# First recurrent part: inverse rows on GpSimd, unscaled keys, plain value transposes, centred outputs, a split last inverse level, new orders

## The reference

```python
q, k, v = silu(conv4(xn @ W))            # causal depthwise convolution of 4 taps, each
k = k * 128 ** -0.5
alpha, beta = sigmoid(xn @ Wa + ba), sigmoid(xn @ Wb + bb)
def step(S, t):                          # S: batch x head x 128 x 128
    err = S k_t - v_t
    S = alpha_t * S - beta_t * err k_t^T
    return S, S q_t
o = (o - mean(o)) * rsqrt(var(o) + 1e-5) * ln_w + ln_b     # over the 128 values of a head
out = (o * sigmoid(xn @ Wg)) @ Wo
```

## Time and profile before

| | |
|---|---|
| median of 3 runs | 3200.43 us |
| profiled execution | 3194.02 us, span 3192.2 us |
| granted clock, mean | 0.995 |
| busy over the span | TensorE 97%, VectorE 69%, ScalarE 50%, GpSimd 30% |
| chain that ended last | TensorE 81%, VectorE 9%, GpSimd 4%, without a seen wait 3%, ScalarE 2% |
| recurrence of layer 0 | about 400 to 1875 us |

### The profile page before, as it was taken

The page is one execution under the profiler, slowest core; times in us unless marked ns, Lnnn a source line. Parts: engine busy times, 40 slices in busy tenths (PEclk is TensorE's granted clock), DMA queues, the critical chain, the costliest instruction groups (busy, mean ns, idle before and its releaser), DMA issues.

```text
span 3192.2 us, 61403 instructions
## 1 busy us (share of the span) xinstructions
PE 3112.1 (97%) x24240; PEld 2595.8 (81%) x24240; DVE 2204.3 (69%) x4430; ACT 1583.7 (50%) x3464; POOL 949.7 (30%) x1359
## 2 busy tenths in 40 slices
PE   8999989999999999999999989999999999999999
PEld 6888878888888888888888878778888888888887
DVE  6112288888888888888888843665666676666666
ACT  4221356766676667766766653344343333222222
POOL 2322313323332333233323234422323332222212
PEclk9999999999999999999999999999999999999999
DMA  2100211112111111111111145411010111000004
GB/s 91 30 20 27 68 54 48 41 48 54 45 41 53 52 48 42 48 54 45 41 54 51 30 157 158 140 43 30 27 30 27 30 43 30 27 20 27 24 17 158
DMA packets 130241, 165.69 MB, mean 52 GB/s; under 512 B 9937, under 2 KB 72145, under 8 KB 129921
## 3 DMA queue, kind: packets, MB, share of 16 engines
q1 hardware_dynamic: 120592, 144.49, 15.1%
q10 hardware_dynamic: 9296, 17.04, 1.5%
q0 software_dynamic: 64, 0.23, 0.0%
HBM read 127.91 MB, written 33.82 MB: 51 GB/s over the span
## 4 chain that ended last, share of the span: by engine, by line
PE 81%; DVE 9%; POOL 4%; issue 3%; ACT 2%; DMA 1%; DVEq 0%; ACTq 0%; SPq 0%; POOLq 0%
PE bank L71 21%; PE bank L73 21%; PE bank L72 21%; PE bank L932 3%; DVE b_zt L1430 3%; PE bank L1045 2%; PE bank L1071 2%; PE bank L1055 2%; PE bank L944 2%; PE bank L1070 1%; PE bank L1030 1%; PE bank L1020 1%; PE bank L1081 1%; DVE b_MN L1500 1%; POOL b_ss L1708 1%
## 5 line engine op out<-in xcount | busy, mean ns | idle before, releaser
L1430 DVE SCALAR_TENSOR_TENSOR b_zt<-b_rx,b_cw,b_zt 128x512 f32<-128x512 f32 x576 | 483.7, 840 | 29.7 <-ACT b_zt L1193 9.7
L71 PE MATMUL bank<-b_XH,b_wh 128*128 128x512 f32 x1024 | 465.4, 455 | 0.0
L72 PE MATMUL bank<-b_XL,b_wh 128*128 128x512 f32 x1024 | 404.0, 395 | 0.0
L73 PE MATMUL bank<-b_XH,b_wl 128*128 128x512 f32 x1024 | 403.4, 394 | 0.0
L71 PE MATMUL bank<-b_XH,b_qh 128*128 128x512 f32 x1024 | 399.3, 390 | 1.4 <-DVE b_g L2540 1.4
L72 PE MATMUL bank<-b_XL,b_qh 128*128 128x512 f32 x1024 | 398.7, 389 | 0.0
L73 PE MATMUL bank<-b_XH,b_ql 128*128 128x512 f32 x1024 | 398.6, 389 | 0.0
L2639 POOL TENSOR_TENSOR b_QHL<-b_qhd,b_QHH 128x512 fp32r<-128x512 f32 x128 | 181.8, 1424 | 476.6 <-ACT b_QHH L2418 474.2
L2418 ACT CAST b_QHH<-b_qhd 128x512 fp32r<-128x512 f32 x128 | 79.5, 623 | 308.0 <-PE bank L73 186.4
L73 PEld LDWEIGHTS bank<-b_XH,b_wl 128*128 128x128 f32 x1024 | 192.6, 188 | 43.6
L71 PEld LDWEIGHTS bank<-b_XH,b_qh 128*128 128x128 f32 x1024 | 192.5, 188 | 41.6 <-DVE b_g L2540 1.9
(11 more groups left out here) (248 smaller groups left out, 7596.7 us busy)
## 6 DMA issues: line engine op xcount, KB each, us to landing
b_abc<-tmp_a SPq DMA_DIRECT2D x64, 256.0 KB, 4.0
b_gbc<-tmp_g SPq DMA_DIRECT2D x64, 256.0 KB, 3.7
tmp_og<-b_gg SPq DMA_DIRECT2D x64, 256.0 KB, 2.3
b_mo<-tmp_og SPq DMA_DIRECT2D x64, 256.0 KB, 3.2
b_wr<-in_Wk SPq DMA_DIRECT2D x16, 256.0 KB, 4.3
b_wr<-in_Wq SPq DMA_DIRECT2D x16, 256.0 KB, 3.0
b_wr<-in_Wv SPq DMA_DIRECT2D x16, 256.0 KB, 2.9
b_wr<-in_Wg SPq DMA_DIRECT2D x16, 256.0 KB, 3.0
```

Source lines behind the costliest of these rows:

```text
L71: e.do.matmul(out, wh, xh, start=first and k == 0, stop=False)
L72: e.do.matmul(out, wh, xl, start=False, stop=False)
L73: m = e.do.matmul(out, wl, xh, start=False, stop=last and k == n - 1)
L1430: e.do.scalar_tensor_tensor(out=z[:, :], in0=rx[:, j:j + 512], scalar=cw[:, u // 2, KIND[name[0]], j:j + 1], in1=z[:, :], op0=ALU.mult, op ...
```

## The change

- rows moves from VectorE to GpSimd, unchanged.
- Keys are left without the factor 128 ** -0.5: finish writes them straight to KQA, scaled_k goes, and the step sizes are scaled by 1/128 in the stage ahead instead.
- The values are transposed only; the mean is taken from the outputs: ScalarE's copy of the outputs is two activations with a sum each, sums squares the centred values through scale and bias, mean (GpSimd) divides the sums, and scaled subtracts and multiplies, in four operations a batch instead of one.
- inverse7 and inverse8 are done in three calls: 7 for chunks 0 to 3; 8 for 0 to 3 and 7 for 4 to 7 in turn; 8 for 4 to 7. out7 is in two halves.
- The orders of all five engines in a round, the banks and the lags are new. g1 is projected a round later; the decay of queries and off_diagonal a round (by its index) sooner.

```diff
-PROJECTIONS = (("v1", 1), ("g0", 2), ("k0", 0), ("v0", 0), ("g1", 2), ("q0", 0), ("k1", 0), ("q1", 0))
+PROJECTIONS = (("g1", 3), ("q0", 1), ("k1", 1), ("q1", 1), ("v1", 1), ("g0", 2), ("k0", 0), ("v0", 0))
 
 TURNS = (
-    ("sc0", 1, 0), ("s6", 2, 3), ("s7", 2, 3), ("sc1", 1, 1), ("turn0", 3, 0), ("sc2", 1, 3),
-    ("s8", 2, 2), ("sc3", 1, 1), ("turn1", 3, 2), ("kv3", 2, 1), ("kv0", 1, 0), ("kv1", 1, 0),
-    ("kv2", 1, 3), ("s3", 1, 0), ("s4", 1, 0), ("s5", 1, 1),
+    ("kv0", 2, 2), ("kv1", 2, 1), ("kv2", 2, 0), ("s3", 2, 1), ("s4", 2, 1), ("s5", 2, 0),
+    ("s6", 2, 2), ("sc0", 1, 3), ("s7a", 2, 0), ("s78", 2, 2), ("sc1", 1, 1), ("sc2", 1, 3),
+    ("turn0", 3, 0), ("kv3", 2, 1), ("sc3", 1, 2), ("turn1", 3, 0),
...
-            m = e.do.matmul(kb[:, x * 256 + 128:x * 256 + 256], t[f"vt{b}"][:, (c0 + x) * 128:(c0 + x + 1) * 128], cmat,
-                            start=True, stop=True)
+            m = e.do.transpose(kb[:, x * 256 + 128:x * 256 + 256], t[f"vt{b}"][:, (c0 + x) * 128:(c0 + x + 1) * 128], ident)
...
+    def inverse7(u, m):
+
+        return e.do.matmul(bank[BANK["s7a"]][64:128, m * 64:m * 64 + 64], X[0:64, m, 64:128], NF[0:64, m, :], start=True, stop=True)
+
+    def inverse8(u, m):
+        return e.do.matmul(bank[BANK["s78"]][0:64, m * 64:m * 64 + 64], Z2[64:128, m, :], t[f"MF{u % 2}"][64:128, m, 64:128],
+                           start=True, stop=True)
+
+    def inverse7_first(u):
+        if not live(u):
+            return
+        bank_free(e, "s7a", u)
         e.wait_ge("mfc", 6 * u + 2)
         e.wait_ge("mfd", 3 * u + 3)
-        for m in range(8):
-            r = e.do.matmul(bank[BANK["s7"]][64:128, m * 64:m * 64 + 64], X[0:64, m, 64:128], NF[0:64, m, :], start=True, stop=True)
+        for m in range(4):
+            r = inverse7(u, m)
         r.then_inc(S["s7"], 1)
 
-    def inverse8(u):
-        if not live(u):
-            return
-        bank_free(e, "s8", u)
-        e.wait_ge("z2", u + 1)
+    def inverse78(u):
+
+        if not live(u):
+            return
+        bank_free(e, "s78", u)
+        e.wait_ge("z2", 2 * u + 1)
         e.wait_ge("mfc", 6 * u + 6)
-        e.wait_ge("mfd", 3 * u + 3)
-        for m in range(8):
-            r = e.do.matmul(bank[BANK["s8"]][0:64, m * 64:m * 64 + 64], Z2[64:128, m, :], t[f"MF{u % 2}"][64:128, m, 64:128],
-                            start=True, stop=True)
+        for m in range(4):
+            inverse8(u, m)
+            r = inverse7(u, m + 4)
+        r.then_inc(S["s7"], 1)
+
+    def inverse8_second(u):
+        if not live(u):
+            return
+        e.wait_ge("z2", 2 * u + 2)
+        for m in range(4, 8):
...
-            e.do.activation(z[:, :], z[:, :], ACT.Silu, bias=bias).then_inc(S["ksil"], 1)
+            e.wait_ge("p1", chain_step(u - 2, 3)[1])
+            e.do.activation(KQA[:, u % 2, b, :, :], z[:, :].rearrange("p (c t) -> p c t", c=4), ACT.Silu, bias=bias).then_inc(S["kq"], 1)
...
-        e.do.copy(t["OS"][:, :, ch, :], bank[7][:, 0:256].rearrange("p (b t) -> p b t", b=2)).then_inc(S["oc"], 1)
+        for b in range(2):
+            i = 4 * b + ch
+            e.do.activation(t["OS"][:, b, ch, :], bank[7][:, b * 128:b * 128 + 128], ACT.Copy,
+                            accum_out=t["ss"][:, 3, i:i + 1]).then_inc(S["oc"], 1)
...
-            e.do.activation(t["sq"][:, :], t["OS"][:, b, ch, :], ACT.Square,
-                            accum_out=t["ss"][:, 0, i:i + 1]).then_inc(S["sqs"], 1)
+            e.do.activation(t["sq"][:, :], t["OS"][:, b, ch, :], ACT.Square, scale=-128.0,
+                            bias=t["ss"][:, 3, i:i + 1], accum_out=t["ss"][:, 0, i:i + 1]).then_inc(S["sqs"], 1)
...
-    def scaled_k(u, b):
-        if not live(u):
-            return
-        e.wait_ge("ksil", 2 * u + b + 1)
-        e.wait_ge("p1", chain_step(u - 2, 3)[1])
-        e.do.tensor_scalar(KQA[:, u % 2, b, :, :], t[f"zt{(6 * u + 3 * b) % 2}"][:, :].rearrange("p (c t) -> p c t", c=4),
-                           KS, None, ALU.mult).then_inc(S["kq"], 1)
...
-        e.do.tensor_tensor(t["OS"][:, b, :, :], t["OS"][:, b, :, :], ss[:, 2, b * 4:b * 4 + 4].unsqueeze(2).to_broadcast([128, 4, 128]),
-                           ALU.mult).then_inc(S["osc"], 1)
+        e.wait_ge("mu", u + 1)
+        for ch in range(4):
+            i = 4 * b + ch
+            r = e.do.tensor_scalar(t["OS"][:, b, ch, :], t["OS"][:, b, ch, :], ss[:, 4, i:i + 1], ss[:, 2, i:i + 1], ALU.subtract, ALU.mult)
+        r.then_inc(S["osc"], 1)
...
+        e.do.tensor_scalar(ss[:, 4, :], ss[:, 3, :], 1.0 / 128, None, ALU.mult).then_inc(S["mu"], 1)
...
```

More of the change, by code:

```diff
@@ new lines, in attn0_pe @@
+        project(i - 1, "k1", 0, 1)
+        project(i - 1, "q0", 1, 2)
+        chain1(i - 3, 3)
+        ahead(i - 3, 2)
+        project(i - 1, "q0", 2, 3)
+        project(i - 1, "k1", 1, 2)
+        project(i - 1, "q0", 3, 4)
+        chain2(i - 3, 3)
+        ahead(i - 3, 3)
+        project(i - 1, "k1", 2, 3)
+        turn_kv(i - 2, 2)
+        project(i - 1, "k1", 3, 4)
+        chain4(i - 3, 3)
+        project(i - 1, "q1", 0, 1)
+        chain3(i - 3, 3)
+        ahead(i - 3, 4)
+        inverse3(i - 2)
```

353 lines of the change are left out of this document (173 added, 180 removed), and 6 rows, old and new, of tables (EMPTIED, SEMAPHORES).

## The result

The changed kernel takes 3222.39 us (median; 3220.09 to 3225.61) against 3200.2 us: a ratio of 1.0059 with a 95% interval of 1.004 to 1.0079. It is slower, by about 22 us, or 0.6%, where 46 us less had been forecast. The profiled execution took 3221.71 us with a span of 3219.9.

What follows compares the result with a forecast made beforehand. TensorE (98% busy) was taken as the bound. New work 42.25 us plus 1.8 of stall gives a period of 44.05 against 45.48, -46 us over 32 rounds: 3149 us, with 8 in 10 from 3095 to 3230.

Steps and rivals of the forecast that it cites:

- TensorE's saved work: Value transposes 0.9 us less a round, inverse7 and inverse8 interleaved 0.25 less: 1.15 x 32 = 37 us.
- Its whole work: TensorE's instructions in one round summed to 43.4 us before the change and 42.25 after it.
- The rows on GpSimd: The 30 row operations on GpSimd take 15.0 us a round, plus 0.8 for halo and tail copies.
- 1.4 us of new stall a round before inverse3: On TensorE: rows and copies want 15.8 us where 14.4 are left, so inverse3 waits.
- Rival B: GpSimd becomes the bound, rows at 25 us delay spread, blocks and inverse3: 3344 us; chance 0.17.
- about 2.1 us of each round is TensorE waiting: Kernel before: round of 45.48 us less 43.4 of work, mostly waits before the outputs' turn and third scores.
- the old stall: TensorE's wait before scores 2 for masked, behind scaled and the root: 0.4 us a round stays.
- I take nothing: VectorE's scaled as eight operations for two: bounds -0.7 to +0.9 us a round, priced at no change.
- Filling and draining: Start and end of the kernel: 35 rounds in both, the round starts elsewhere; plus or minus 8 us.
- C: Rival: cuts eaten by waits at ScalarE or slow rows, 3178 to 3207 us; chance 0.13 together with D.
- D: Rival: interleaved batch doesn't overlap, value transposes no cheaper, 3194 us; chance 0.13 together with C.
- A: Rival: rows at 11.4 to 13 us, no stall but 0.4, period 42.65, 3103 us; chance 0.23.

Runs made afterwards that it cites:

- e1: Changed kernel with one root step instead of four (12 of 16 small GpSimd operations left out): 3155.16 us.
- e9: Kernel before the change with one root step instead of four: 3155.23 us.
- g4: Changed kernel with the last 7 of the 15 row steps on GpSimd left out: 3209.55 us.
- e4: Changed kernel with the 30 row operations put back on VectorE, in the new order: 3293.59 us.
- e5: Changed kernel with one wait added, so GpSimd's product of queries and decay starts only after scaled: 3199.4 us.
- e2: Changed kernel with scaled as one multiplication a batch as before, the subtraction of the mean left out: 3198.2 us.
- e3: Kernel before with the value part alone (transposed values, mean from output copies, scaled in eight operations): 3215.15 us.
- g3: Changed kernel with the query-decay product waiting for scaled, the weight cut behind the root and first_guess ahead of added4: 3185.9 us.
- g2: Changed kernel with one root step instead of four and the query-decay product waiting for scaled: 3166.19 us.

## Why the prediction was wrong

**TensorE's saved work: right. Its whole work: 1 us a round too small.** The value transposes stand 0.11 us apart, and the interleaved batch of inverse7 and inverse8 starts its 16 small matmuls within 0.46 us, so they overlap. e1 against e9 has 0.97 us less of work for 1.15 forecast. But the sum of 43.4 us for the round of before was too small. e9, where TensorE waits for 0.02 us a round, takes 44.17. The kernel before waits in every second round only:

```profile
PE bank L932 <- issue: 14.5, 14, 1.0
PE bank L1081 <- DVE b_XPA L1461: 11.8, 14, 1.0
```

That is TensorE's whole wait from 461.5 to 1825.9 us but for 0.5, so 0.9 us a round, not 2.1. The prediction read one round with 1.8 us of waits and took it for each. The largest term that it had too small is the 96 projection matmuls: 22.1 us by a rounded 0.23, 24.4 from start to start in e9.

**The rows on GpSimd: right, and safer than forecast.** GpSimd's timeline has the first and the last of a unit:

```profile
1068.88 0.22 POOL L1703 TENSOR_TENSOR b_PR<-b_A,b_T 128x15 f32<-128x15 f32 x1 [6.19 <-issue]
...
1082.14 0.58 POOL L1706 TENSOR_TENSOR b_T<-b_T,b_PR 128x15 f32<-128x15 f32 x1
```

13.84 us to 1082.72, for 15.0 forecast. The block transposes follow at 1084.98 and inverse3 at about 1088, so the "1.4 us of new stall a round before inverse3" was not there (0.04), nor in e1, whose round is 2 us shorter. Rival B, which decided from 17.2 us of rows and copies, named the right sign for a mechanism that did not act: g4 and e4 speak against it.

**The steps that failed: "about 2.1 us of each round is TensorE waiting" and "the old stall".** The first put the new round's work at 42.25 where it is 43.35. The second priced the wait before the scores at 0.4 us a round; it is 1.15. Its root was right: 7.4 us and 1.4 more with a cut, 7.3 and 8.6 measured, the same on both kernels. Its scaled was not: 1.5 us behind the root's end, from "I take nothing", where the trace shows 3.1. The bounds of 0.1 to 0.3 us an operation hold for seven of the eight (0.26 from start to start); the remaining one stands still for GpSimd's product (1.34 us), which starts right behind the root. The prediction saw that product there ("now fall among decay and masked") and priced it for decay only. e5 is the test: with the product kept away no operation is held, and 23 us of the kernel come back. e2 shows the same with two operations, e3 with the weight cut in place of the product. The Trainium skill, page "SBUF — State Buffer", section "Who interferes with whom", would have warned here: it lists `tensor_scalar` among the operations that can, under conditions on their operands, take the port pair that VectorE has in common with GpSimd, and says that whoever comes first then keeps the other out for a whole instruction. The trace agrees: 1303 ns against 332 to 346, ending 0.08 us after the product. That which was cited for the rows was not applied to the new operations.

**What was not priced: the clock.** After 2.2 us of idle the granted clock was 0.66 and 0.83 in the windows above, 1.7 us lost. From 400 us to the end of the recurrence the stretches at the 1.2 GHz level sum to 51 us after and 17 before, 20 in e1, 7 in e9, 27 in g3. In the 30 rounds alone they are 27 us after and 14 before, 0.46 and 0.23 us a round at half speed, and none in e1, e9, e5 and g3.

**What was not foreseen: stops inside inverse4.** 0.5 us a round after (15.3 us in 30 rounds), none before, where inverse3 and inverse4 stood 2.7 us apart and now 1.1.

**Filling and draining: "plus or minus 8 us" was +17** (7.6 + 9.1). With the granted clock at 0.91, 0.77 and 0.97 in 1842 to 1860, 1860 to 1880 and 1880 to 1901, (0.09 x 18) + (0.23 x 20) + (0.03 x 21) = 6.9 of the drain's 9.1 us could be clock, where before had 1.00 throughout. e1's drain is nearly as long and has a lowered clock too, 0.74 in its middle 20 us (5.2 us); e9's has 1.00. While it fills, the kernel after has 0.87 from 430 to 469 us and the one before 0.94 from 430 to 461: 5.1 against 1.9 us. So up to 3.2 + 6.9 and, in the rounds, 0.23 x 30 = 6.9, together 17 of the 27.7 us of span, stand beside a lowered clock. That is an upper bound, since TensorE is not busy all the time where it fills and drains.

**The sum.** TensorE's waits of the kernel after from 469.1 to 1842.2 us, the four largest and inverse3:

```profile
PE bank L938 <- DVE b_XPA L1482: 34.6, 28, 2.5
PE bank L978 <- issue: 8.0, 9, 1.4
PE bank L975 <- issue: 7.3, 8, 1.5
PE bank L70 <- ACT b_gg L1367: 3.8, 7, 0.7
PE bank L963 <- DVE b_MN L1507: 1.0, 6, 0.2
```

Forecast period 42.25 + 1.8 = 44.05. Measured 45.77: 1.96 of idle (1.15 before the scores, 0.51 in inverse4, 0.13 for the gates, 0.03 before inverse3, 0.14 small), 0.46 of clock (the lowered stretches at half speed, an upper bound), and the rest, 43.35, is work. So the waits in all came near the 1.8 forecast, by luck: a stall of 1.4 that did not come made room for ones that were not foreseen. Against the kernel before (44.36 of work, 0.90 of idle, 0.23 of clock) the work fell by 1.0, and the idle grew by 1.06 and the clock's share by 0.23, where the prediction had the waits fall by 0.3.

**The rivals.** C's region (3178 to 3207) is nearest, for another reason (its upper end is a slip: a period of 45.7 gives 3194 + 7 = 3201); D didn't act; A would have needed a root path that isn't late: even with a short root the kernel takes 3155, not 3103. One of the prediction's signs of being wrong did show: TensorE's longest idle is elsewhere, before the scores.

## What to carry to other kernels

When work leaves the engine that is not the bound, look for the serial path that the bound waits on, and price every link of it with what the engine next door does at that moment; here one operation of 1.34 us placed in the middle of eight small ones cost 23 us, a lowered clock included. Before a wait seen in one round is put into a sum, count in how many rounds it is there: here it was every second one, and the work that the sum made of it was 1 us too small. Look at the spread of durations, not only at the mean: a mean of 458 ns was seven of 340 and one of 1300. A wait that keeps two such operations apart can pay (e5, and g3 with 3185.9 us), but only while the protected path is the late one (g2). Where the path was made short in both kernels, the rest of the change showed its net worth: here nothing, 3155.16 against 3155.23, since half of the saved work went into stops inside inverse4 and the rest into filling and draining.
